# A state-space mixer and a ternary feed-forward on one core: merged column operations, a moved down product, a separate last output buffer

## The reference

```python
def activation_quant(x):                       # one scale for each row
    s = 127 / clip(max(abs(x), axis=-1), 1e-5)
    return clip(round(x * s), -128, 127) / s
def bit_linear(x, w):                          # weight_quant(w): mean(abs(w)) * {-1, 0, 1}
    return einsum('bsh,oh->bso', activation_quant(x), weight_quant(w))
h = silu(bit_linear(xn, w_gate)) * bit_linear(xn, w_up)     # xn = layernorm(x)
h = ln_weight * h * rsqrt(mean(h * h) + 1e-6)
x = x + bit_linear(h, w_down)
```

## Time and profile before

| | |
|---|---|
| runs, us | 586.08, 587.4, 585.56; median 586.08 |
| profiled execution, us | 586.31 |
| its span, us | 584.4 |
| busy share of the span | PE 93%, DVE 92%, ACT 88%, POOL 79%, PEld 69% |
| mean granted TensorE clock | 0.991 of full |

### The profile page before, as it was taken

How to read it: one execution, slowest core, us unless ns; L and a number is a source line. 1 busy time by engine, 2 the same in 40 slices (tenths; PEclk the granted TensorE clock), 3 DMA queues, 4 the chain that set the end, 5 groups by cost and what they waited for, 6 DMA issues and landing times.

```text
span 584.4 us, 10287 instructions
## 1 busy us (share of the span) xinstructions
PE 541.3 (93%) x3667; PEld 404.7 (69%) x3684; DVE 540.5 (92%) x820; ACT 512.1 (88%) x755; POOL 464.5 (79%) x184
## 2 busy tenths in 40 slices
PE   5898987999999999999999888998889999999996
PEld 2335476899998989989999888995334444444442
DVE  3999979999999999999999999997998999999873
ACT  1899999999999999989999799998967868778673
POOL 4888374999999899999999999994564765666662
PEclk9999999999999999999999899899999999999998
DMA  9992690221112741127331194234532533424321
GB/s 285 407 364 73 230 309 11 56 65 64 55 55 91 163 117 65 59 63 202 88 98 55 55 228 168 62 128 106 104 65 63 109 81 78 112 65 97 94 54 55
DMA packets 62194, 68.65 MB, mean 117 GB/s; under 512 B 41136, under 2 KB 41136, under 8 KB 59968
## 3 DMA queue, kind: packets, MB, share of 16 engines
q1 hardware_dynamic: 59776, 63.59, 36.3%
q0 software_dynamic: 2368, 4.40, 4.5%
HBM read 50.02 MB, written 8.52 MB: 100 GB/s over the span
## 4 chain that ended last, share of the span: by engine, by line
DVE 28%; PE 26%; ACT 17%; POOL 12%; issue 11%; DMA 5%; SPq 0%; DVEq 0%; POOLq 0%; ACTq 0%
POOL arena L470 11%; ACT arena L682 8%; PE ps L1221 8%; PE ps L1205 6%; ACT arena L607 5%; DVE arena L808 5%; PE ps L1208 4%; PE ps L1263 4%; PE ps L1256 3%; DVE arena L897 3%; DVE arena L985 3%; DMA arena<-arena 2%; DVE bst_x L840 2%; DVE am L954 1%; DMA arena<-x 1%
## 5 line engine op out<-in xcount | busy, mean ns | idle before, releaser
L470 POOL TENSOR_TENSOR arena<-arena 128x2048 f32<-128x2048 f32 x63 | 286.4, 4592 | 13.2 <-DVE arena L897 11.1
L897 DVE TENSOR_TENSOR_SCAN arena<-arena,ps 128x512 f32<-128x512 f32 x256 | 286.7, 1197 | 2.0 <-ACT arena L682 0.5
L682 ACT ACTIVATE arena<-arena,a_neg 128x512 f32<-128x512 f32 x256 | 165.5, 712 | 9.5 <-DVE arena L897 9.2
L1221 PE MATMUL ps<-ident,arena 128*128 128x128 f32 x1024 | 156.0, 276 | 6.7 <-POOL arena L470 3.4
L1221 PEld LDWEIGHTS ps<-ident,arena 128*128 128x128 f32 x1024 | 121.2, 142 | 10.7 <-POOL arena L470 6.2
L504 POOL TENSOR_TENSOR arena<-arena 128x1024 f32<-128x1024 f32 x30 | 71.1, 2371 | 57.2 <-DVE arena L985 57.2
L1256 PE MATMUL ps<-arena 128*128 128x512 bf16 x504 | 112.9, 379 | 2.1 <-DVE arena L985 1.1
L1205 PE MATMUL ps<-arena 128*128 128x128 f32 x768 | 102.3, 276 | 3.4 <-ACT arena L607 2.1
L1208 PE MATMUL ps<-ident,arena 128*128 128x128 f32 x640 | 97.8, 277 | 5.2 <-DVE arena L897 2.9
L607 ACT ACTIVATE arena<-arena,bT 128x512 f32<-128x512 f32 x160 | 102.0, 711 | 0.0
L1205 PEld LDWEIGHTS ps<-arena 128*128 128x128 f32 x768 | 93.3, 192 | 5.2 <-ACT arena L607 2.3
(11 more groups left out here) (121 smaller groups left out, 578.1 us busy)
## 6 DMA issues: line engine op xcount, KB each, us to landing
arena<-w_all SPq DMA_DIRECT2D x16, 1024.0 KB, 9.2
arena<-c_rows SPq DMA_DIRECT2D x64, 256.0 KB, 3.2
arena<-x SPq DMA_DIRECT2D x4, 1024.0 KB, 15.8
w_ternary<-arena SPq DMA_DIRECT2D x8, 512.0 KB, 4.2
arena<-w_ternary SPq DMA_DIRECT2D x8, 512.0 KB, 5.0
arena<-x POOLq DMA_DIRECT2D x4, 1024.0 KB, 10.0
out<-arena SPq DMA_DIRECT2D x16, 256.0 KB, 2.0
arena<-ctx_t SPq DMA_DIRECT2D x4, 512.0 KB, 13.7
```

The lines of the kernel that those rows point to most:

```text
L470: nc.gpsimd.tensor_tensor(hs[:, k % RING, :, :], hs[:, k % RING, :, :], c_bc[:, s:s + 1, :].to_broadcast([P, KE, L]), ALU.mult).then_inc(S ...
L682: nc.scalar.activation(dA[:, s, i, :], delta_u[:, b, 0, i, :], ACT.Exp, scale=a_neg[:, i, n:n + 1]).then_inc(S["dA_ready"], 1)
L897: nc.vector.tensor_tensor_scan(out=hs[:, k % RING, i, :], data0=dA[:, k % 2, i, :], data1=ps[:, 4 + i, :], initial=0.0, op0=ALU.mult, op1= ...
L1221: last = mm(ps[:, c, i * P:(i + 1) * P], hs[:, k % RING, i, c * P:(c + 1) * P], ident[:], start=(n == 0 and i == 0), stop=(n == DS - 1), i ...
```

## The change

The change has these parts.

- `scale_row`: the row maximum is clamped and divided by 127 in one operation; both columns of `scales` come from one operation on `wmean[:, 0:2]`; `s1` is the reciprocal and signals by itself. Two column operations fewer.
- `variance`: the factor `scales[:, t, 1:2]` squared, until now two multiplications on DVE, goes into the `Square` on ACT as its `scale`, a column read from memory; one column operation fewer. The same for the last tile (two fewer).
- `bias` moves from DVE to POOL, behind `power`. It waits for `power` and for the norm of the tile before; DVE waits for it before it overwrites `mv`.
- `down(END - 2)`, tile 13, moves on PE from behind chunk 2 of tile 15 to behind `turn_end(END - 1)`; `scale_rows(END - 2)` on ACT moves behind the scaling L774 of the last tile.
- The last output rows get their own buffer `o_end`, and L1063 no longer waits for an earlier store.

```diff
+        o_end = part(124, 2)
...
-                sp.dma_start(out_v[:, t, :], o_s[:, t % 2, :]).then_inc(out_stored[t % 2], 16)
+                sp.dma_start(out_v[:, t, :], o_end if t == END else o_s[:, t % 2, :]).then_inc(out_stored[t % 2], 16)
...
+            def bias(t):
+                pool.wait_ge(S["rstd_ready"], t + 1)
+                hold(pool, "xn_ready", t)
+                nc.gpsimd.tensor_scalar(bia[:], mv[:, 0:1], rstd2[:, 0:1], -1.0, ALU.mult,
+                                        ALU.mult).then_inc(S["bias_ready"], 1)
...
                         power(n // 4 + 1, 0, 1)
+                        bias(n // 4)
...
                     power(EARLY + t + 1, 0 if tile(t + 3) else 1, 2 if tile(t - 1) else 1)
+                if tile(t + 3):
+                    bias(t + 3)
...
-                    nc.scalar.activation(sq_out, h2[:, 1 - s, :], ACT.Square,
+                    nc.scalar.activation(sq_out, h2[:, 1 - s, :], ACT.Square, scale=scales[:, t - 1, 1:2],
...
                     nc.scalar.activation(sq_out[:, 0:1024], h2[:, END % 2, 0:1024], ACT.Square,
+                                         scale=scales[:, END, 1:2],
...
-                if tile(t - 2):
+                if tile(t - 2) and t < END:
                     scale_rows(t - 2)
...
-            nc.scalar.activation(sq_out[:, 1024:], h2[:, END % 2, 1024:], ACT.Square,
+            nc.scalar.activation(sq_out[:, 1024:], h2[:, END % 2, 1024:], ACT.Square, scale=scales[:, END, 1:2],
...
+            scale_rows(END - 2)
             act.wait_ge(S["qT_psum"], 2)
...
                     step(nc.vector.bn_stats(bst[:], x_all[:, n, :]))
+                    hold(dve, "bias_ready", n)
                     own.done(nc.vector.bn_aggr(mv[:], bst[:]))
                 if chain is not None:
                     dve.wait_ge(S["ssq_ready"], chain + 1)
-                    own.done(nc.vector.tensor_scalar(var2[:, 1:2], ssq[:, chain:chain + 1], scales[:, chain, 1:2],
-                                                     1.0 / INNER, ALU.mult, ALU.mult))
+                    own.done(nc.vector.tensor_scalar(var2[:, 1:2], ssq[:, chain:chain + 1], 1.0 / INNER, RMS_EPS,
+                                                     ALU.mult, ALU.add))
                 own.wait()
                 if n is not None:
-                    own.done(nc.vector.tensor_scalar(var2[:, 0:1], mv[:, 1:2], LN_EPS, None, ALU.add))
-                if chain is not None:
-                    own.done(nc.vector.tensor_scalar(var2[:, 1:2], var2[:, 1:2], scales[:, chain, 1:2], RMS_EPS,
-                                                     ALU.mult, ALU.add))
-                own.wait()
+                    step(nc.vector.tensor_scalar(var2[:, 0:1], mv[:, 1:2], LN_EPS, None, ALU.add))
                 dve.sem_inc(S["var_ready"], 1)
-
-            def bias(n):
-                dve.wait_ge(S["rstd_ready"], n)
-                nc.vector.tensor_scalar(bia[:], mv[:, 0:1], rstd2[:, 0:1], -1.0, ALU.mult,
-                                        ALU.mult).then_inc(S["bias_ready"], 1)
...
-                step(nc.vector.tensor_scalar(am[:], am[:], Q_EPS, None, ALU.max))
-                own.done(nc.vector.reciprocal(s1[:], am[:]))
-                for w in range(2):
-                    own.done(nc.vector.tensor_scalar(scales[:, x, w:w + 1], wmean[:, w:w + 1], am[:], 1.0 / 127.0,
-                                                     ALU.mult, ALU.mult))
-                own.wait()
-                step(nc.vector.tensor_scalar(s1[:], s1[:], 127.0, None, ALU.mult))
-                dve.sem_inc(S["s1_ready"], 1)
+                step(nc.vector.tensor_scalar(am[:], am[:], Q_EPS, 1.0 / 127.0, ALU.max, ALU.mult))
+                step(nc.vector.tensor_scalar(scales[:, x, :], wmean[:, 0:2], am[:], None, ALU.mult))
+                nc.vector.reciprocal(s1[:], am[:]).then_inc(S["s1_ready"], 1)
...
-            step(nc.vector.tensor_scalar(var_end[:], ssq[:, END:END + 1], scales[:, END, 1:2], 1.0 / INNER, ALU.mult,
-                                         ALU.mult))
-            own.done(nc.vector.tensor_scalar(var_end[:], var_end[:], scales[:, END, 1:2], RMS_EPS, ALU.mult, ALU.add))
+            step(nc.vector.tensor_scalar(var_end[:], ssq[:, END:END + 1], 1.0 / INNER, RMS_EPS, ALU.mult, ALU.add))
             dve.wait_ge(S["ssq_end_ready"], 1)
-            own.done(nc.vector.tensor_scalar(ssq_end[:], ssq_end[:], scales[:, END, 1:2], 1.0 / INNER, ALU.mult,
-                                             ALU.mult))
-            own.wait()
-            step(nc.vector.tensor_scalar(var2[:, 1:2], ssq_end[:], scales[:, END, 1:2], var_end[:], ALU.mult, ALU.add))
+            step(nc.vector.tensor_scalar(var2[:, 1:2], ssq_end[:], 1.0 / INNER, var_end[:], ALU.mult, ALU.add))
...
-            dve.wait_ge(out_stored[END % 2], END // 2 * 16)
-            nc.vector.scalar_tensor_tensor(out=o_s[:, END % 2, :], in0=ps[:, DOWN_BANK[END % 2], :],
+            nc.vector.scalar_tensor_tensor(out=o_end, in0=ps[:, DOWN_BANK[END % 2], :],
...
+            def turned_by_dma(t):
+                pe.wait_ge(qT_done[t % 2], (t // 2 + 1) * 16)
...
-                    if j == 2 and tile(t - 2):
-                        pe.wait_ge(qT_done[t % 2], ((t - 2) // 2 + 1) * 16)
+                    if j == 2 and tile(t - 2) and t < END:
+                        turned_by_dma(t - 2)
                         pe.wait_ge(S["wd_cut"], 4)
                         down(t - 2, 0, KI)
...
             turn_end(END - 1, ps_q, 0)
+            turned_by_dma(END - 2)
+            down(END - 2, 0, KI)
             pe.wait_ge(S["qT_copied"], 1)
             down(END - 1, 0, 8)
```

More of the change, by code:

```diff
@@ L995, in _ @@
                         variance(t, None)
-                    if b == NB - 1 and n % 4 == 2 and t < EARLY:
-                        bias(t + 1)
             dve.wait_ge(S["p_ready"], LAST)
@@ L1023, in _ @@
                     scale_row(x_row)
-                if tile(t + 3):
-                    bias(EARLY + t + 1)
                 if tile(t):
```

## The result

The changed kernel takes 588.75 us (median of 22 runs, 585.13 to 591.33), the kernel before in the same comparison 586.14 (22 runs, 583.95 to 587.64). The ratio is 1.0043, 95% interval 1.0028 to 1.0058: slower by 0.43%, some 2.5 us. The forecast was 585.3, range 583.4 to 587.3, most probably no change. It was wrong: the measured time lies above the range.

A forecast was written before the change was run, and what follows sets the result against it. Three close limits per feed-forward tile: an ACT-DVE dependency loop 10.61 us, DVE 10.56, PE 10.37. From 586.31, minus 2.2 up to down(12), plus 1.4 at the end, gave 585.5; 0.2 lower for the median, 585.3, range 583.4 to 587.3.

The forecast's parts named there:

- The ring: Steady feed-forward tile, a dependency loop through ACT and DVE: period from 10.61 to 10.52 us, by -0.18 and +0.09.
- The pointer: Square on ACT, its scale read from memory: 0.09 us more per tile, bounds 0 and 0.19, inside the tile's dependency loop.
- the gain to down(12): Feed-forward up to tile 12's down product: 0.9 + 0.8 + 0.5 = 2.2 us sooner, bounds 1.4 and 3.0.
- the long landing: Before down(1), one DMA transpose took 5.9 us, median 4.4; if repeated the gain there is 0.55, otherwise 1.2.
- two operations 0.19 + 0.24: In `scale_row` on DVE, after the 0.72 reduction: 0.24 for the two-column operation; whole stretch 1.25 to 1.3, saving 0.5 us.
- down(0) starts where it did, to within 0.3: End of the scan part: delay from bias on POOL is absorbed by the 0.5 us `scale_row` gives, so tile 0's down product keeps its start.
- At full clock the move gives 0.15: Last tiles on PE: with down(13) moved, tile 15's transposes start at 575.65 instead of 575.80 us.
- The term +1.35: Net cost in us of moving down(13): 1.5 lost to low clock after 3.6 idle on PE, less 0.15 gained.
- the rival in which it holds: End of the kernel: PE's clock holds despite 3.6 us idle, or its low stretch falls into that idle time; 583.8 us, chance 0.12.
- bias(2): Scan part, third bias operation on POOL: on the path, +0.35 us, perhaps 0.15 back from the shorter `scale_row`.
- The slower one: End of the kernel: PE stays at 1.2 GHz from tile 14's transposes through down(13) and down(14); 591.6 us, chance 0.10.
- The rival in which the gain doesn't come: Steady part: POOL's bias costs 0.7 and more, a slow transpose recurs; main part -0.5, end +1.4; 587.0 us, chance 0.14.

The follow-up runs named there:

- e7_both_back: The changed kernel with two one-column operations for `scales` again and down(13) with `scale_rows(13)` in their old places: 584.35 us, ratio 0.9976 against the kernel before.
- e4_down_back: The changed kernel with down(13) and `scale_rows(13)` back in their old places, the merged two-column operation kept: 585.43 us, ratio 0.9993 against the kernel before.
- e13_bias_pool: The kernel before with one edit, bias(0) to bias(2) of the scan part on POOL behind its power: 585.81 us, ratio 1.0020.
- e1_two_ops: The changed kernel with the two columns of `scales` written by two one-column operations again: 588.1 us, ratio 1.0035 against the kernel before.
- e6_widths: The kernel before plus unread DVE multiplications one, two or three columns wide behind every second scan step of two batches; run once for its trace, no time given.
- e3_merge_only: The kernel before with only the two one-column operations of `scales` merged into one of two columns: 591.63 us, ratio 1.0077.

## Why the prediction was wrong

**Right.** The ring: forecast 10.52, measured 10.52. The pointer: 0.09, confirmed a second time by its doubling. `variance`: 0.49 forecast, 0.48. POOL's operation: 0.25 plus a hop of 0.11, measured 0.26 (L483 ends at 470.45, L489 starts at 470.56). Counted from the end of POOL's last product, down(0) stood where it did to 0.2, and the gain to down(12), 2.2 forecast within 1.4 to 3.0, is 2.63; counted from the start of the span the scan's loss ate it. The gain came earlier than written: 1.7 at down(1), since the long landing of the earlier trace rows didn't recur, and less in the last turns. `scale_row` with `bias` gone gave 0.3 (L958 to L984 1.48, before 1.78) and not 0.5, which nothing waited for. Put together and measured without the two bad edits (e7_both_back), the rest gains 1.4 us (0.4 to 2.4), where 2.2 was forecast; the 0.3 at the very end and the scan's bias, named above, are open parts of the difference.

**Failed step 1: "two operations 0.19 + 0.24".** The two-column operation was priced by its size, and the text names nothing that it could wait for. Measured: 0.45 to 0.47 in the feed-forward, up to 2.72 in the changed kernel's scan part and 5.19 in the merge alone, set by POOL's running product. It was not in the sum, and no rival had it, although the operation stood in a stretch where the prediction itself had counted POOL's products "without a pause". So "down(0) starts where it did, to within 0.3" failed as well: the scan part took 2.3 us more. By e4_down_back and e7_both_back the merge is worth about 1.0 us here; alone it cost 4.5. The runs show the wait and its end; which part of the chip is shared they don't show. The Trainium skill (SBUF — State Buffer, Who interferes with whom) has the rule: VectorE and GpSimd share one pair of ports, a VectorE operation in a two-port mode takes it, and whoever comes second is fully blocked. The Trainium skill (VectorE: DVE Perf Modes, What auto-detection actually checks) adds that such a mode needs one source, all in SBUF, and outermost dimensions of more than one that are even or equal. A column alone has no such dimension, so by this it never waits. The traces agree: 0.19 to 0.21 us for one column, up to 6.08 for two, and 0.36 to 0.39 for three.

**Failed step 2: the end, "At full clock the move gives 0.15".** The term +1.35 came to 3.2 (2.2 to 4.2), and both halves of it were mis-sized. The order: I set PE's 575.65 against 575.80 of the earlier trace rows. But 575.80 is itself a T15 behind a down(14) at the lower clock (5.31 us), and I took the second half of the rows (575.4) as the time of all of them, while the first eight transposes need only the first half, ready at 574.34 (573.65 + 0.69 in the timeline of L1057). At full clock the old order has T15 6.62 us behind T14, not 7.94; the new order has 7.8, since PE has 32 matmuls between. The order costs 1.2 us. The clock: taken as 1.5 against an execution that had paid 1.3 itself (7.94 against 6.62). In the new order it costs 1.3 (9.14 against 7.8) or 2.8 (10.55) where it drops, and nothing in one profile of three; in the old order it dropped in three profiles of eight. Busy matmuls in the idle time returned 1.7 us, with intervals that overlap. In the profiled pair the term came out at +1.35 only because that execution of before had the low clock too.

The sum took the clock to drop ("3.6 will") and gave the rival in which it holds 0.12. Two of three profiles with the idle time show the drop; one shows none (idle 3.60, clock 1.00 in the whole of T14 to T15). By the Trainium skill (TensorE: Matmul & The Clock Gate, Part 1) an idle PE goes to half rate, and the two agree with it.

**Mis-sized, and small:** bias(2), +0.35 and perhaps 0.15 back, is 0.5 in the trace of e13_bias_pool, which is no more than two executions of the same scan differ by; whether the runs pay more is open, as told above.

**The rivals.** The slower one (the lower clock through T14, down(13) and down(14), 591.6) named the right place and the right direction, but 8.2 us of low clock as the point from which it decides, where 3.4 or 6.8 were enough, since the order itself cost 1.2 and the port 1.0. As a ladder from before to the changed kernel: -1.4 for the rest, +1.0 for the merge, +2.9 for the move on top is +2.5, the result. These are steps between neighbouring ratios, so they must add up and prove nothing by it. What does not follow from them is that the move alone costs 3.2 on the kernel before, and 3.5 between e7_both_back and e1_two_ops. The merge is not so steady: 4.5 alone, 1.0 in the old order, and 0.5 between e1_two_ops and the changed kernel. The rival in which the gain doesn't come, 587.0, had the wrong cause.

## What to carry to other kernels

Merging two one-column operations on VectorE into one of two columns isn't free of risk: look whether GpSimd runs then, since the pair may wait for the whole of its operation, and in a part tied to GpSimd the singles at 0.2 us each are cheaper. Even in the feed-forward here the merged one took 0.46 us, and two singles together 0.34. Before a term is set against "before", check at which clock that stretch of the profiled execution ran, and which half of the data the waiting step really needs. Work moved from behind one wait into the next leaves PE idle ahead of it; the order must pay for itself at full clock first, and the clock comes on top in some executions.

## What the runs showed of the hardware

- VectorE multiplications by a scalar (`tensor_scalar`) of two float32 columns in SBUF, begun while GpSimd ran a product, ended 0.02 to 0.04 us behind the end of a product (five in e6_widths, 0.38 to 6.08 us long). Those of three columns took 0.36 to 0.39 and ended so too. Those of one column take 0.19 to 0.21 us whatever GpSimd does.
- The waiting operation isn't always next: in e3_merge_only (5.19 us) GpSimd's next product began 0.30 us after it and was finished first, and in e6_widths that happened twice (5.33 and 6.08 us).
- Idle times of 3.48 to 3.60 us on TensorE were followed by 0, 3.4 and 6.8 us at the lower clock in three executions with the same order of work. With 15 matmuls in the idle time the one profile shows none, and the mean granted clock over the runs was 0.9929, against 0.9886.
- A stretch at the lower clock appeared in the common first part (80.7 us) in the changed kernel's profile and not in that of before: +1.45 us that belong to no edit. In e7_both_back the first scan came 2.9 us later than before, also with low clock ahead of it.
